# Moving a query's sums of squares to the end of TensorE's step, with a signal of its own for the turned keys

## The reference, cut to what matters

```python
def rms_norm(x, w):
    var = jnp.mean(jnp.square(x), axis=-1, keepdims=True)
    return x * jax.lax.rsqrt(var + EPS) * w
q = rms_norm(latents @ Wq, q_norm_w); k = rms_norm(kv @ Wk, k_norm_w); v = kv @ Wv
probs = softmax(einsum('bhgqd,bhkd->bhgqk', q, k) / sqrt(128))
out = einsum('bhgqk,bhkd->bhgqd', probs, v) @ Wo
```

## Time and profile before

| | |
|---|---|
| median of three runs | 2357.87 us |
| profiled execution: its own time, its span | 2362.0 us, 2360.2 us |
| mean granted clock of TensorE | 0.97 |
| busy over the span: PE, DVE, ACT, POOL | 2163.2, 1713.1, 1252.0, 206.0 us |
| stage A, steps 0 to 63 | about 465 to 1255 us of the span |
| stage B, steps 0 to 63 | about 1676 to 2270 us of the span |
| PE and DVE busy from 454 to 1260 us | 773.9 and 590.2 of 806 us, granted clock 0.99 |
| PE and DVE busy from 1675 to 2275 us | 566.7 and 526.9 of 600 us, granted clock 0.98 |

### The profile page before, as it was taken

The page is one execution under the profiler, slowest core; times in us unless marked ns, Lnnn a source line. Parts: engine busy times, 40 slices in busy tenths (PEclk is TensorE's granted clock), DMA queues, the critical chain, the costliest instruction groups (busy, mean ns, idle before and its releaser), DMA issues.

```text
span 2360.2 us, 40918 instructions
## 1 busy us (share of the span) xinstructions
PE 2163.2 (92%) x15200; PEld 1263.9 (54%) x15200; DVE 1713.1 (73%) x4385; ACT 1252.0 (53%) x3519; POOL 206.0 (9%) x211
## 2 busy tenths in 40 slices
PE   4897999999999999999986797999899999999878
PEld 2554444456666666666653454444555555555444
DVE  6675555777777777777768666667788989888873
ACT  3664211466666666666643565334666666666521
POOL 3662000000000000000000354000000000000010
PEclk8999999999999999999997999999999999999989
DMA  4000212010010000100000000111011011011000
GB/s 181 19 11 3 70 36 74 34 46 19 28 45 20 28 19 28 46 19 11 28 18 19 19 19 20 54 63 46 8 39 46 30 44 46 19 46 40 19 1 36
DMA packets 10709, 82.16 MB, mean 35 GB/s; under 512 B 1424, under 2 KB 1424, under 8 KB 3088
## 3 DMA queue, kind: packets, MB, share of 16 engines
q1 hardware_dynamic: 10512, 79.54, 9.4%
HBM read 77.44 MB, written 2.10 MB: 34 GB/s over the span
## 4 chain that ended last, share of the span: by engine, by line
PE 49%; DVE 28%; ACT 12%; issue 8%; POOL 2%; DMA 0%; SPq 0%; ACTq 0%; DVEq 0%; POOLq 0%
PE bank L561 41%; ACT probs L1402 5%; DVE probs L2000 3%; ACT pT_hi L1461 3%; DVE rawmax L1968 3%; DVE pT_lo L2038 2%; DVE qT_lo L1906 2%; PE bank L949 2%; DVE wa_lo L1558 1%; PE bank L932 1%; DVE oT_lo L2012 1%; PE bank L672 1%; DVE masked L1976 1%; DVE kn L1896 1%; DVE wo_lo L1558 1%
## 5 line engine op out<-in xcount | busy, mean ns | idle before, releaser
L561 PE MATMUL bank<-xnT_hi,wa_hi 128*128 128x512 f16 x736 | 279.4, 380 | 3.7 <-PE bank L561 2.6
L561 PE MATMUL bank<-xnT_lo,wa_hi 128*128 128x512 f16 x736 | 279.4, 380 | 0.0
L561 PE MATMUL bank<-xnT_hi,wa_lo 128*128 128x512 f16 x736 | 279.2, 379 | 0.0
L561 PE MATMUL bank<-wo_hi,oT_hi 128*128 128x512 f16 x576 | 225.1, 391 | 25.3 <-DVE oT_lo L2012 16.8
L1402 ACT ACTIVATE probs<-bank,negmax,rms_r 128x256 f32<-128x256 f32 x256 | 141.2, 561 | 185.9 <-DVE negmax L1973 185.9
L561 PE MATMUL bank<-wo_lo,oT_hi 128*128 128x512 f16 x576 | 224.6, 390 | 0.0
L561 PE MATMUL bank<-wo_hi,oT_lo 128*128 128x512 f16 x576 | 224.1, 389 | 0.0
L561 PE MATMUL bank<-wa_hi,xnT_hi 128*128 128x512 f16 (+3 forms) x640 | 204.4, 325 | 4.5 <-DVE xnT_lo L1622 2.4
L561 PE MATMUL bank<-wa_lo,xnT_hi 128*128 128x512 f16 (+3 forms) x640 | 203.9, 324 | 0.0
L561 PE MATMUL bank<-wa_hi,xnT_lo 128*128 128x512 f16 (+3 forms) x640 | 203.8, 324 | 0.0
L2038 DVE TENSOR_TENSOR pT_lo<-bank,pT_hi 128x512 f16<-128x512 f32 x192 | 126.8, 688 | 45.0 <-ACT pT_hi L1461 37.5
(11 more groups left out here) (274 smaller groups left out, 5517.9 us busy)
## 6 DMA issues: line engine op xcount, KB each, us to landing
raw<-in_w_qkv_dram SPq DMA_DIRECT2D x18, 1536.0 KB, 6.6
raw<-in_w_out_dram SPq DMA_DIRECT2D x18, 1024.0 KB, 4.9
raw<-in_w_ffn_dram SPq DMA_DIRECT2D x15, 1024.0 KB, 4.9
raw<-in_w_ffn0d_dram SPq DMA_DIRECT2D x7, 512.0 KB, 3.5
x<-in_x_dram SPq DMA_DIRECT2D x4, 512.0 KB, 5.7
expert_b<-in_expert_b_dram SPq DMA_DIRECT2D x1, 2048.0 KB, 9.4
raw<-in_w_ffn3b_dram SPq DMA_DIRECT2D x2, 1024.0 KB, 4.9
out_dram<-x SPq DMA_DIRECT2D x1, 2048.0 KB, 6.3
```

The lines of the kernel that those rows point to most:

```text
L561: mm = pe.matmul(dst, l, r, start=start and k == 0, stop=stop and k == n - 1)
```

## The change

The sums of squares go from bank KV to bank O from unit 5 on. `sum_q` moves behind the second half of `out_proj`, to the end of PE's step. `turn_k` signals `w_kT` in every step, and ACT's `kT_hi` waits for that. `mean_q` moves on DVE from behind `kT_lo` to the head of the next step, before the maxima. PE's wait for `mean_q` moves from `project_kv` to `attend`, which overwrites bank O. Stage B's `out_proj` is cut two and two heads.

```diff
-            return bank[S1 if p < 3 else Y if p < 5 else KV]
+            return bank[S1 if p < 3 else Y if p < 5 else O]
@@ PE: project_kv, attend, turn_k, out_proj
-                    if s >= 1 and s + 4 < UNITS:
-                        pe.wait_ge(w_meanq, U + 5)
                     for j in range(tiles):
@@
                 def attend(U, s):
                     pe.wait_ge(w_plo, U)
+                    if s + 4 < UNITS:
+                        pe.wait_ge(w_meanq, U + 5)
@@
-                    if s < 0 or s + 5 >= UNITS:
-                        mm.then_inc(w_kT, 1)
+                    mm.then_inc(w_kT, 1)
@@
-                    early = 2 if tiles == 2 else 3
+                    early = 2 if tiles == 2 else 2
@@ PE: step
-                    if s < UNITS - 5:
-                        sum_q(U, s)
                     if s >= 1:
                         out_proj(U, s, 1)
                         if (s - 1) % B == B - 1:
                             pe.wait_ge(w_out, U)
                             pe.sem_inc(out_used, 1)
+                    if s < UNITS - 5:
+                        sum_q(U, s)
@@ ACT: prologue and step
-                    act.wait_ge(w_kT, n * 5 + 1)
+                    act.wait_ge(w_kT, U + 1)
@@
-                        if s + 5 < UNITS:
-                            act.wait_ge(w_sums, U + 6)
-                        else:
-                            act.wait_ge(w_kT, n * 5 + s - (UNITS - 5) + 2)
+                        act.wait_ge(w_kT, U + 2)
@@ DVE: prologue and step
-                    mean_q(4)
@@
+                    if has_q:
+                        mean_q(s + 4)
                     maxima()
@@
-                    if s + 5 < UNITS:
-                        mean_q(s + 5)
```

## The result

The changed kernel takes 2326.47 us (median of 4 runs, 2326.21 to 2332.19), the kernel before 2357.87 (4 runs): ratio 0.9873, 95% interval 0.9856 to 0.9890. It is faster, as forecast, but by 31.4 us where 23.6 were forecast, and it lies under the low end of the range, 2328. A second series, with both kernels on another occasion, gave 2327.92 against 2357.31, ratio 0.9877 (0.9862 to 0.9892).

The account below looks back on a forecast made before the run. PE is busiest, but DVE's loop through `kT_hi` sets stage A's steps and PE stalls for `kT_lo` in B; 18.8 us from A plus 4.8 from B make 23.6, so 2357.87 becomes 2334 us, range 2328 to 2344.

Parts of the forecast that it names:

- Stage A's loop: DVE's loop through `kT_hi` ends last in stage A; shortened by 0.43 us net, plain steps 11.69, stage gain 18.8 us.
- part (2): Stage A: `mean_q` ahead of the maxima costs DVE's loop 0.08 us, bounds 0.07 and 0.15.
- Stage B's step: Stage B: plain step 8.78 us against 8.79, gaining nothing, as the wait for `kT_lo` is traded for one for `v_lo`.
- Attend behind `mean_q`: `attend`'s new wait stays hidden in B, `mean_q` seen at 1.57 us, 0.42 to spare; slower rival 2368 us, chance 0.02.
- part (2) of stage B: Stage B: large-piece steps fall to 8.78, seven octets gain 5.8 us, last steps without queries lose 1.0; net 4.8.
- 2 for the prologue and spells of the lower clock: Allowance of 2 us, outside the repeating steps, taken off 2330 to reach the low end 2328.
- the drained step: Steps 32 (A) and 24 (B), PE waiting for its own last matmul: 0.46 us extra, kept unchanged in the forecast.
- stage A's last steps: Last eight steps of stage A: hardly any stall left to take, so only seven octets counted, gain 0.
- what lies outside the stages: Everything outside stages A and B: forecast change 0.

Follow-up runs that it names:

- the three copies: Changed kernel with three further copies of `mean_q`, written to scratch, at the head of DVE's step: 2333.63 us against 2357.31, ratio 0.9905.
- The first experiment: Changed kernel with stage B's output projection cut three and one heads again, as in the kernel before: 2323.61 us against 2361.52, ratio 0.9837.
- before again: The kernel before, unchanged, profiled once more: span 2355.2 us, execution 2357.08 us; median of 10 runs 2360.68.
- the signal only: Kernel before with only the turned keys' own signal for `kT_hi` and the sums in bank O: 2330.19 us against 2361.52, ratio 0.9867.
- three then two: Changed kernel with stage B cut three and one heads in steps 0 to 58, two and two in the last five: 2316.89 us, ratio 0.9829.
- keys waiting for sums: Changed kernel, but ACT's `kT_hi` waits for the sums of squares again, with `sum_q` still at the end of PE's step: 2478.23 us, one run.

## Why the prediction was right and wrong

**Stage A's loop: right.** `kT_hi` starts 0.94 us after `v_lo` does (0.95 forecast), `mean_q` costs 0.07. Rows of the timeline at the end of step 34 and the head of step 35, where the earlier trace rows stood:

```profile
878.83 0.41 DVE L1895 SCALAR_TENSOR_TENSOR v_lo<-bank,v_hi 128x256 f16<-128x256 f32 x1
879.30 0.44 PE L938 MATMUL bank<-const,kn 128*128 128x128 f32 x2
...
879.77 0.38 ACT L1453 ACTIVATE kT_hi<-bank 128x256 f16<-128x256 f32 x1 [0.37 <-PE bank L938]
...
883.24 0.15 DVE L1915 TENSOR_SCALAR rms_a<-bank 128x4 f32<-128x4 f32 x1
883.31 0.68 DVE L1963 TENSOR_REDUCE rawmax<-bank 128x2 f32<-128x512 f32 x1
```

**The price weighed in part (2): 0.07, not the full 0.15.** The instructions of four numbers last 0.15 us and cost 0.07 each, in the row above and in the three copies. At their full time the copies would have made large-piece steps 12.27 us (estimate: 11.82 and three times 0.15); they took 12.02. The Trainium skill, page VectorE: DVE Perf Modes, section The DRAIN you can't avoid, says that the next instruction doesn't start until the pipe is empty, but also that one that is not held starts earlier. The prediction took only the first half and so read the page as a rule against this part; the rows agree with the second.

**Stage B's step: right, and so is the finding that its plain step gains nothing.** The turn waits for `v_lo` in all 56 steps. The first experiment shows the consequence: three and one is 6.65 us better there.

**Attend behind `mean_q`: right.** In the changed kernel no wait of `attend` for `rms_a` shows. In step 26 of stage B the masking starts 1.19 us after the scores (1885.71 from 1884.52), so `mean_q`, which stands right before it, is seen at some 1.3, ahead of the 1.57 forecast; the copies moved it by 0.21 with no cost in B.

**The step that failed, part (2) of stage B: "between 0 and 1.8 us lost, I take 1.0" for its last steps, and the low end's "2 for the prologue and spells of the lower clock".** Steps 56 to 62 gained 1.9 to 3.2 us. I counted matmuls behind the turn and didn't look at what PE's wait for `oT_lo` does to its clock. Three matmuls moved from ahead of `probs_T` to behind the turn cost next to nothing, as there is slack, and shorten the idle stretch from 2.3 to 1.9 us; the clock of steps 59 to 62 rises from 0.87 (0.91 in before again) to 0.95. The same cut taken back only there costs 4.4 us. So the term had the wrong sign: a gain of 2 to 3 in place of a loss of 1.

**Mis-sized: the drained step.** PE's wait for its own last matmul cost 0.46 us ahead of the scores and costs 0.31 ahead of `sum_q` (12.13 against 11.82, and 9.10 against 8.79), 0.15 an octet in either stage, 2.1 us in all that I left out. Net, steps 0 to 55 gave 1.4 to 1.5 more than forecast, as steps 0 to 7 of stage A fell short of their 2.7.

**Also left out:** stage A's last steps (1.2 to 2.8 us), put at nothing on the word of step 57 alone, while steps 59, 60 and 62 of the kernel before took 13.09, 12.78 and 12.77; and what lies outside the stages (1.5 to 3.7), which ranges from 1017.2 to 1021.4 us over all profiles and from 1017.2 to 1019.3 over those of the changed kernel and its variants, so that 1.5 of it says nothing. In both executions of the kernel before a stretch at the lower clock fell into step 59 of stage A, in both of the changed kernel none did, but the one with four means had it again (13.18 us against 11.68), and so had the signal only (12.91). Why it falls there or not wasn't separated; with PE's idle time filled, steps 59 to 62 of stage A had none, in one profile.

From before again to after the profiles differ by 30.7 us, 7.1 more than forecast: 2.9 in stage B's last steps, 1.5 in steps 0 to 55, 1.2 in stage A's last steps and 1.5 outside the stages. The first is the largest, and the only one of them with the wrong sign.

## What to carry to other kernels

When an engine waits for a semaphore, ask what it needs and what else that semaphore counts: here `kT_hi` waited for sums that it didn't read, and its own signal gave as much in the repeating steps as the whole change. Before a cover is moved, look from both sides: the matmuls that covered `kT_lo` had covered `v_lo`. In a tail where the matmul engine has less work, the length of its idle stretches can matter more than its work, and the cut that is right for the body (three and one) may be wrong for the tail (two and two): taken together they gave 2316.89 us, 0.9829 of the kernel before, against 0.9877 for the changed kernel beside it. Only the kernels with unread matmuls are as fast (0.9828 and 0.9823).

## What the runs showed of the hardware that was not expected

Eight unread matmuls a step, 1.7 us each time, made steps 59 to 62 of stage B 4.3 us shorter in all (38.98 to 34.65): the granted clock stayed at 2.4 GHz when PE's idle stretch fell from 2.3 to 0.6 us. With idle stretches of 1.9 us these steps had no time at the lower clock in two kernels (three then two, and keys waiting for sums) and a granted clock of 0.95 in two others (the changed kernel, and the one with the copies of `mean_q`); what makes the difference is open.
